# Moving the running-state update ahead of the first value product, and splitting one PSUM eviction in two, in an attention and feed-forward layer on eight cores

## What is computed

```python
qkv = x @ Wqkv_w.T + Wqkv_b          # q, k, v with 16 heads of 64
k = k * scale
scores = einsum('bhld,bhmd->bhlm', q, k)
y = einsum('bhlm,bhmd->bhld', scores * causal, v)
x = layernorm(x + y @ out_w.T + out_b)
h = silu(x @ wg.T) * (x @ wu.T)       # wg, wu, wd = int / 127
x = layernorm(x + h @ wd.T)
```

## Time and profile before

| | us |
|---|---|
| device time, median of two executions | 2186.61 (2182.42 and 2190.81) |
| device time of the profiled execution | 2188.3 |
| span of the profiled execution, slowest core (core 3) | 2186.7 |
| spans of the eight cores | 2156.9 to 2186.7 |
| PE busy on core 3 | 1815.5 |
| DVE, ACT, POOL busy on core 3 | 407.3, 400.8, 284.9 |
| PE's granted clock over the span, by core | 0.909 to 0.918 |

### The profile page before, as it was taken

The page is one execution under the profiler, slowest core; times in us unless marked ns, Lnnn a source line. Parts: engine busy times, 40 slices in busy tenths (PEclk is TensorE's granted clock), DMA queues, the critical chain, the costliest instruction groups (busy, mean ns, idle before and its releaser), DMA issues.

```text
span 2186.7 us, 26522 instructions; the slowest of 8 cores (2156.9 to 2186.7 us)
## 1 busy us (share of the span) xinstructions
PE 1815.5 (83%) x9556; PEld 852.8 (39%) x9556; DVE 407.3 (19%) x803; ACT 400.8 (18%) x647; POOL 284.9 (13%) x263
## 2 busy tenths in 40 slices
PE   0785888998778788999768787999978878899985
PEld 0342443443234344444324444444433444444432
DVE  0212121121121212211111222212112121212111
ACT  0130221111013122111002213111101222211101
POOL 2032142100003021000001203000010312100001
PEclk9986989999988788999988788999999788899998
DMA  9119089965620002323551000222362010122354
GB/s 172 20 14 122 1 99 141 166 134 140 177 68 11 30 1 65 86 78 82 162 146 39 20 20 21 92 76 75 111 201 84 1 44 1 30 82 78 85 166 154
DMA packets 127935, 180.01 MB, mean 82 GB/s; under 512 B 58800, under 2 KB 58816, under 8 KB 127424
## 3 DMA queue, kind: packets, MB, share of 16 engines
q1 hardware_dynamic: 73728, 151.03, 24.5%
q0 software_dynamic: 54080, 27.28, 11.5%
HBM read 188.76 MB, written 35.65 MB: 103 GB/s over the span
## 4 chain that ended last, share of the span: by engine, by line
PE 68%; DMA 15%; DVE 5%; issue 5%; POOL 3%; ACT 3%; SPq 0%; DVEq 0%; POOLq 0%; ACTq 0%
PE pF L741 13%; PE pF L733 13%; PE pF L411 11%; PE pF L821 10%; PE pF L593 7%; DMA wdr<-wd_scr 6%; PE pF L470 5%; DMA wu_scr<-wuT 5%; DMA wo_bf<-woT 2%; PE pF L386 2%; PE pF L513 2%; ACT v_tm L478 2%; PE pF L536 1%; DVE h1f L639 1%; PE pF L552 1%
## 5 line engine op out<-in xcount | busy, mean ns | idle before, releaser
L821 PE MATMUL pF<-wdr,h_fm 128*128 128x512 bf16 x1472 | 350.7, 393 | 64.1 <-DMA wdr<-wd_scr 63.0
L733 PE MATMUL pF<-x_fm,wgr 128*128 128x512 bf16 x1536 | 365.6, 381 | 10.5 <-DMA wgr<-wg_scr 6.7
L741 PE MATMUL pF<-x_fm,wur 128*128 128x512 bf16 x1536 | 363.3, 379 | 1.5 <-DMA wur<-wu_scr 1.5
L411 PE MATMUL pF<-x_fm,wqkv_bf 128*128 128x512 bf16 x1024 | 242.3, 402 | 12.9 <-DVE x_fm L396 8.0
L821 PEld LDWEIGHTS pF<-wdr,h_fm 128*128 128x128 bf16 x1472 | 141.4, 100 | 272.5 <-issue 131.3
L755 DVE TENSOR_TENSOR h_fm<-silu_s,pF 128x512 bf16<-128x512 bf16 x192 | 132.0, 688 | 533.3 <-PE pF L741 533.3
L733 PEld LDWEIGHTS pF<-x_fm,wgr 128*128 128x128 bf16 x1536 | 150.0, 98 | 193.2 <-issue 16.2
L741 PEld LDWEIGHTS pF<-x_fm,wur 128*128 128x128 bf16 x1536 | 150.3, 98 | 184.4 <-issue 4.8
L752 ACT ACTIVATE silu_s<-pF 128x512 bf16<-128x512 f32 x192 | 114.6, 597 | 551.1 <-PE pF L733 551.1
L711 POOL TENSOR_SCALAR out_sb<-h1f,stats 128x1024 f32<-128x1024 f32 x32 | 38.2, 1193 | 999.2 <-DVE stats L709 989.0
L692 ACT ACTIVATE sqs<-h1f 128x1024 bf16<-128x1024 f32 x64 | 67.3, 1051 | 544.6 <-DVE h1f L840 397.5
(11 more groups left out here) (79 smaller groups left out, 1026.1 us busy)
## 6 DMA issues: line engine op xcount, KB each, us to landing
wdr<-wd_scr SPq DMA_DIRECT2D x256, 256.0 KB, 3.5
wgr<-wg_scr SPq DMA_DIRECT2D x96, 256.0 KB, 2.6
wur<-wu_scr SPq DMA_DIRECT2D x96, 256.0 KB, 2.7
x_tm<-x SPq DMA_DIRECT2D x32, 512.0 KB, 4.4
out<-out_sb SPq DMA_DIRECT2D x32, 512.0 KB, 3.8
wqkv_bf<-wqkvT POOLq DMA_DIRECT2D x8, 768.0 KB, 24.8
wg_scr<-wgT POOLq DMA_DIRECT2D x24, 256.0 KB, 12.5
wu_scr<-wuT POOLq DMA_DIRECT2D x24, 256.0 KB, 13.4
```

The source lines that it names most:

```text
L411: last = e.matmul(pF[:, b, :], wqkv_bf[:, kc, oc * P:(oc + 1) * P], x_fm[:, kc, :], start=(kc == 0), stop=(kc == DC - 1))
L733: last = e.matmul(pF[:, b, :], wgr[:, slot, kc, :], x1_fm[:, kc, t2 * 512:(t2 + 1) * 512], start=(kc == 0), stop=(kc == DC - 1))
L741: last = e.matmul(pF[:, b, :], wur[:, slot, kc, :], x1_fm[:, kc, t2 * 512:(t2 + 1) * 512], start=(kc == 0), stop=(kc == DC - 1))
L821: last = e.matmul(pF[:, 1 + 2 * j + n2, :], h_fm[:, hc, gc * P:(gc + 1) * P], wdr[:, slot, n2 * 512:(n2 + 1) * 512], start=False, stop=(id ...
```

## The change

Two edits in the chunk loop. First, for chunks with g < 15, `s_upd_f` is given to PE before `y_intra_f(c, g, 0)` and no longer between it and `y_intra_f(c, g, 1)`; its operands and its place after `y_zero_f` are the same. Second, the copy of y from banks 5 and 6 to `y_fm` becomes two ACT instructions of 512 columns, one for each bank. The plan still sees one operation: it waits for the same event of PE before the first, and signals after the second.

```diff
             if c <= 3:
                 pl.op("pe", y_zero_f(), reads=[r_consts],
                       writes=[rb[5], rb[6]])
+                if g < 15:
+                    pl.op("pe", s_upd_f(c, g), reads=[r_k[c], r_v[c]],
+                          writes=[rb[0]])
                 pl.op("pe", y_intra_f(c, g, 0),
                       reads=[r_v[c], r_at_e, r_consts],
                       writes=[rb[5], rb[6]])
-                if g < 15:
-                    pl.op("pe", s_upd_f(c, g), reads=[r_k[c], r_v[c]],
-                          writes=[rb[0]])
                 pl.op("pe", y_intra_f(c, g, 1),
                       reads=[r_v[c], r_at_o, r_consts],
                       writes=[rb[5], rb[6]])
...
                 def y_ev(e):
-                    return e.activation(
-                        y_fm[:].rearrange("p a n -> p (a n)"),
-                        pF[:, 5:7, :].rearrange("p a n -> p (a n)"), AF.Copy)
+                    e.activation(y_fm[:, 0:4, :], pF[:, 5, :], AF.Copy)
+                    return e.activation(y_fm[:, 4:8, :], pF[:, 6, :],
+                                        AF.Copy)
```

## The result

The changed kernel takes 2203.18 us (median of 14 executions), the kernel before 2184.86 (median of 13 beside them). The ratio is 1.007 with a 95% interval of 1.0043 to 1.0098: slower by 0.4 to 1.0%, clear of no change, within 2%. The forecast was 2187.4 in a range of 2174 to 2200, so the time lies outside, on the slow side.

A forecast was written before the change was run, and what follows sets the result against it. The prediction took PE to bound the kernel, busy 1815.5 of 2186.7 us. Its terms, 0 + 0 + 0.8 us on the 2186.6 median, gave 2187.4 us, range 2174 to 2200.

The forecast's parts named there:

- What bounds the kernel; the place of the waits: Whole kernel: PE bounds it, and the moved update can fill only pass 0's mask waits, 27.9 us, not L639's 47.5.
- Part one, pass 0 gains nothing: Pass 0: the update fills the even-mask wait, the odd-mask wait grows as much; at least 3 us shifts, gain nothing.
- Part two, the update costs the same in front: Passes 1 to 3, 22 updates: about 0.4 us each in either place, difference nothing; bounds 11.7 us loss, 9.2 gain.
- The rival that it loses its company: Chunk-loop products: the update in front shares less with neighbouring matmuls; up to 11.7 + 0.8 us slower, chance 0.12.
- hardly more at half the clock: Passes 1 to 3: the update adds 0.42 us at low clock against 0.38 at full, so some matmuls overlap neighbours.
- Part three, the split copy: Copy of y on ACT: two instructions take 0.07 us longer, paid eleven times, 0.8 us in all, 1.9 at most.
- The clock: Loops of tiles 1 to 7: shifted clock switches could gain 26.2 us or lose 7.8; chances 0.14 better, 0.09 worse.
- The sum: Whole kernel: pass 0 nothing, passes 1 to 3 nothing, split copy 0.8 us, giving 2187.4 us from the median.
- the better side: Loops of tiles 1 to 7: one to three tiles join the fast tile 5, time 2173 to 2183 us, chance 0.14.

The follow-up runs named there:

- e4: Kernel before with the update moved ahead of the zero writes, into PE's wait for the residual add, and one copy of y; ratio to before 0.9891.
- e2: Kernel before with only the copy of y split in two instructions, the update still between the products; ratio to before 0.9983.
- e5: Kernel before with the update given to PE after both products, one copy of y; ratio to before 0.9985.
- e1: Kernel before with only the update moved ahead of both products, one copy of y; ratio to before 1.0064.
- e11: Changed kernel with sixteen zero matmuls ahead of the zero writes, in PE's wait for the residual add; ratio to before 0.9887.
- e3: Changed kernel with sixteen zero matmuls of the update's form between the two products, where the update had stood; ratio to before 0.9879.

## Why the prediction was wrong

*What bounds the kernel; the place of the waits*: right. Pass 0 pays the two mask waits, passes 1 to 3 the wait on L639, and the change reached only the first.

*Part one, pass 0 gains nothing*: right. The wait moved from L616 to L627 and their sum with the new wait on L605 stayed (27.9, now 28.1 us). I expected at least 3 us to move; 5.1 left L616, 3.5 came to L627 and 1.8 to L605. Pass 0 is 18.05 us before and 18.11 changed, means of 56.

*Part two, the update costs the same in front*: wrong in size, in the harmless direction. I took nothing between bounds of +11.7 and -9.2. Alone in front it adds 0.25 us and not 0.38, so 22 x 0.13 = 2.9 us at full clock were gained, and 2.69 - 2.41 = 0.28 us a pass at low. The rival that it loses its company falls with the same number. One reading in this part was wrong as well. I took 2.06 us as the block at the low clock and subtracted twice 0.82. But the clock of that pass fell just after the block's start, and the products without the update don't take twice as long at the low clock. Blocks wholly at the low clock take 2.14 us from product to L552 (median), and without the update 1.42 (e4). So the update adds 0.71 us there and not 0.42, nearly twice its 0.38. The inference from "hardly more at half the clock" has no ground.

*Part three, the split copy*: right. L676 takes 591 ns behind a 597, the wait of L579 rose by 0.5 us (forecast about 0.6), and e2 can't be told from before.

*The clock*: the step that failed. The sum puts this term at nothing. I saw that 4.8 us a tile hang on when the clock switches and that the change shifts this, and priced it by the loops that the profile held: at worst 302.8, all seven at 43.25, a loss of 7.8, with a chance of 0.09. The loss measured in the loops is 13.1 us, mean of eight cores. The bound was none. It took the slowest loop seen as the slowest there is, but in none of those seven loops were passes 1 and 2 both long: six have one long pass, tile 5 has none. The changed kernel has both long in 28 of its 56 loops, and these last near 46 us. The price that this trace could have given was in the passes: a pass 1 of 13.94 at 0.63 and a pass 2 of 10.77 at 0.84 do nearly the same work, so a loop with both long is 43.20 + 3.2 = 46.4 us, and seven of them are 325, a loss of 30. I also called the direction open, in favour of the better side, "since most tiles are now on the slow side". What I should have asked is what the change takes away between PE's stand and the point where the clock is regained or not. It takes sixteen matmuls' worth of work to the front of that stretch and shortens the stretch by 0.13 to 0.28 us. By e5 the shortening alone costs little; the order is what costs.

*What stays open.* Why the update at the front of the block loses the clock and at its end doesn't (e1 against e5, equal blocks, 27 against 12 long passes 2), when sixteen matmuls still further ahead, in the stand, bring it back (e4, e11), is not settled. It may be that both hold the clock for different reasons: the one keeps it from falling, the other lets it return. No run separates that.

## What to carry to other kernels

Where an engine's clock switches inside a loop, price a reordering by what it does to the clock of each pass, not by the busy time that it moves; the worst loop in the profile is no bound if its passes differ. Try independent PE work first where PE stands and waits for another engine: here the update one statement further up than the change put it, ahead of the zero writes, was 1.1% faster than before and not 0.7% slower. And before counting a shorter PE stretch as a gain, look for the clock that it may lose: sixteen matmuls by zeros made this kernel faster.

## What the runs showed of the hardware that I had not expected

Sixteen matmuls of 64 columns that alternate between the column halves start within 0.25 us at full clock, 16 ns apart, when no product runs beside them (changed kernel, e1, e4). Between the products of the two halves they started within 0.38 us, 25 ns apart (before).

PE's granted clock fell to 0.50 again in passes 1 and 2 (before, core 3, at 1856.24 and 1869.89 us) though PE's stand ahead of L524 is only 1.56 us there in the median. In the changed kernel sixteen zero matmuls in that stand left 1.18 us of it and took the clock of passes 1 and 2 from 0.709 to 0.921 (e11); between the products, with the stand as it was, they took it to 0.919 (e3). Multiplying by zeros counts as work for this.
